# Sums over the partitions in the mixer: one 32-bit matmul becomes two float32r matmuls

## The reference

```
h   = layernorm(x) * (1 + ca) + sa
q, k, v = split(rms(h) @ w_qkv.T);  q = rms(q);  k = rms(k)
y   = sigmoid(q) * cumsum(exp(k) * v) / (cumsum(exp(k)) + 1e-6)
u, g = split(y @ w_swiglu.T)
x   = x + ga * (h + (u * silu(g)) @ w_out.T)
```

## Time and profile before

| | us |
|---|---|
| median of 3 runs | 2037.17 |
| lowest and highest | 2035.51, 2041.21 |
| span of the profiled execution | 2036.9 |
| PE busy in the span | 1888.6 (93%) |
| DVE, ACT, POOL busy | 1382.7, 921.8, 959.1 |
| mixer, steady: PE busy from 450 to 600 | 148.00 of 150 |

### The profile page before, as it was taken

The page is one execution under the profiler, slowest core; times in us unless marked ns, Lnnn a source line. Parts: engine busy times, 40 slices in busy tenths (PEclk is TensorE's granted clock), DMA queues, the critical chain, the costliest instruction groups (busy, mean ns, idle before and its releaser), DMA issues. The chain is left out here.

```text
span 2036.9 us, 25294 instructions
## 1 busy us (share of the span) xinstructions
PE 1888.6 (93%) x8376; PEld 826.3 (41%) x8376; DVE 1382.7 (68%) x1795; ACT 921.8 (45%) x1421; POOL 959.1 (47%) x680
## 2 busy tenths in 40 slices
PE   4638999999999999999999999998999999999996
PEld 1213444444444444444444444443443433433432
DVE  6996884884874866777678457245657768768756
ACT  4445334333423433523432421122776776776773
POOL 0553422421522521431441231213889889989974
PEclk7869999999999999999999999998999999999998
DMA  8223012012012012101101101313101011011011
GB/s 308 83 68 95 24 35 81 11 39 93 5 40 95 6 35 67 40 26 54 62 26 37 60 6 47 112 35 127 63 1 63 22 42 63 22 42 62 0 42 62
DMA packets 62147, 112.06 MB, mean 55 GB/s; under 512 B 4464, under 2 KB 20848, under 8 KB 61424
## 3 DMA queue, kind: packets, MB, share of 16 engines
q1 hardware_dynamic: 62064, 111.06, 16.3%
HBM read 80.11 MB, written 30.93 MB: 55 GB/s over the span
## 5 line engine op out<-in xcount | busy, mean ns | idle before, releaser
L532 PE MATMUL bank<-Y,wsw 128*128 128x512 f16 x3072 | 684.0, 379 | 8.7 <-DVE late L843 8.4
L786 POOL TENSOR_TENSOR late<-late 128x512 f16<-128x512 f32 x128 | 192.1, 1501 | 633.1 <-ACT late L661 633.0
L532 PEld LDWEIGHTS bank<-Y,wsw 128*128 128x128 f16 x3072 | 299.0, 98 | 376.6 <-DVE late L843 12.0
L1621 DVE SCALAR_TENSOR_TENSOR f_A<-bank,gu_s,f_A 128x512 f32<-128x512 f32 x352 | 260.7, 741 | 177.8 <-ACT f_A L1445 166.8
L509 PE MATMUL bank<-late,wout 128*128 128x512 f16 x1536 | 352.4, 379 | 3.6 <-POOL late L786 3.5
L1445 ACT ACTIVATE f_A<-bank,gu_s 128x512 f32<-128x512 f32 x352 | 241.6, 687 | 157.6 <-PE bank L1370 139.1
L487 PE MATMUL bank<-H,wqkv 128*128 128x512 f16 x1152 | 260.1, 387 | 37.0 <-DVE H L868 30.9
L1525 POOL TENSOR_TENSOR f_A<-f_A 128x512 f32<-128x512 f32 x176 | 253.9, 1443 | 72.9 <-DVE f_A L1621 72.4
L1335 PE MATMUL bank<-f_HH,f_down_hi 128*128 128x512 f16 x704 | 267.3, 382 | 20.2 <-POOL f_HH L1535 19.7
L843 DVE TENSOR_TENSOR late<-late,bank 128x512 f32<-128x512 f32 x128 | 87.7, 685 | 227.4 <-PE bank L532 206.8
L653 ACT ACTIVATE late<-bank 128x512 f32<-128x512 f32 x128 | 76.4, 597 | 350.1 <-PE bank L532 265.5
(11 more groups left out here) (151 smaller groups left out, 2143.8 us busy)
## 6 DMA issues: line engine op xcount, KB each, us to landing
room<-packed SPq DMA_DIRECT2D x48, 176.0 KB, 2.4
X<-xT SPq DMA_DIRECT2D x8, 1024.0 KB, 6.0
h_scratch<-X SPq DMA_DIRECT2D x8, 1024.0 KB, 4.2
f_X<-x_scratch SPq DMA_DIRECT2D x8, 1024.0 KB, 5.5
f_N<-x_scratch SPq DMA_DIRECT2D x7, 1024.0 KB, 5.5
outT<-f_X SPq DMA_DIRECT2D x7, 1024.0 KB, 4.2
late<-xT SPq DMA_DIRECT2D x24, 256.0 KB, 2.9
HR<-h_scratch SPq DMA_DIRECT2D x24, 256.0 KB, 3.2
```

Source lines behind the costliest of these rows:

```text
L532: mm = nc.tensor.matmul(out[:], wsw[:, pw, k, col:col + P], Y[:, px, k, :], start=(k == 0 and pw == 0 and px == 0), stop=(k == DT - 1 and ...
L786: nc.gpsimd.tensor_tensor(UG[:, j % 2, 1, :], G, UG[:, j % 2, 0, :], ALU.subtract).then_inc(UG_low, 1)
L1621: nc.vector.scalar_tensor_tensor(a, EV[ev_bank(j, m)][:], gu_s[:, which * I_T + j, g:g + 1], a, ALU.mult, ALU.add).then_inc(by_dve, 1)
```

## The change

`reduce` no longer multiplies the 32-bit tile `RS`. GpSimd writes the sum twice more: once as a float32r tile `RH`, by repeating the last addition with a float32r output just ahead of the ordinary one (`round_sum`), and once as the rest `RL = RS - RH` (`rest_of_sum`) after it. TensorE then does two float32r matmuls that accumulate in the same bank. The first waits for `sum_high`, the second for `sum_low`. `ones_r` is a float32r copy of `ones`. This is done in the 39 reductions of the mixer; block 0's three and those of the second half stay as they are.

```
+            def round_sum(kind, b, last):
+                f = FAMILY[kind]
+                nc.gpsimd.tensor_tensor(RH[f][:], RS[f][:], last, ALU.add).then_inc(sum_high[f], 1)
+            def rest_of_sum(kind, b):
+                f = FAMILY[kind]
+                pool.wait_ge(sum_high[f], parted(kind, b) + 1)
+                nc.gpsimd.tensor_tensor(RL[f][:], RS[f][:], RH[f][:].bitcast(F32), ALU.subtract).then_inc(sum_low[f], 1)
...
                 for c in range(2, DT):
+                    if c == DT - 1:
+                        round_sum(kind, b, SQ[f][:, c % 2, :])
                     nc.gpsimd.tensor_tensor(RS[f][:], RS[f][:], SQ[f][:, c % 2, :], ALU.add).then_inc(sq_sum[f], 1)
+                pool.wait_ge(sq_sum[f], 3 * use + 3)
+                rest_of_sum(kind, b)
...
-                if kind == MEAN:
-                    pe.wait_ge(tile_sum, 3 * (b + 1))
-                else:
-                    pe.wait_ge(sq_sum[f], 3 * (nth_squares(kind, b) + 1))
+                pe.wait_ge(sum_high[f], parted(kind, b) + 1)
                 bank_read(kind, b)
-                nc.tensor.matmul(sum_bank(kind, b)[:], ones[:], RS[f][:], start=True, stop=True).then_inc(reduced[f], 1)
+                nc.tensor.matmul(sum_bank(kind, b)[:], ones_r[:], RH[f][:], start=True, stop=False)
+                pe.wait_ge(sum_low[f], parted(kind, b) + 1)
+                nc.tensor.matmul(sum_bank(kind, b)[:], ones_r[:], RL[f][:], start=False, stop=True).then_inc(reduced[f], 1)
```

More of the change, by code:

```diff
@@ L18 @@
 F32 = mybir.dt.float32
+F32R = mybir.dt.float32r
 F16 = mybir.dt.float16
@@ L61, in program @@
         ones = keep("ones", [P, P], F32)
+        ones_r = keep("ones_r", [P, P], F32R)
         eps = keep("eps", [P, 3], F32)
@@ L91, in mixer @@
     mod, ones, eps, bank = v["mod"], v["ones"], v["eps"], v["bank"]
+    ones_r = v["ones_r"]
     SA, CA, GA, GB = v["SA"], v["CA"], v["GA"], v["GB"]
@@ L121, in mixer @@
         RS = [sb("RSx", [P, T], F32), sb("RSqk", [P, T], F32)]
+        RH = [sb("RHx", [P, T], F32R), sb("RHqk", [P, T], F32R)]
+        RL = [sb("RLx", [P, T], F32R), sb("RLqk", [P, T], F32R)]
         RD = sb("RD", [P, 2, T], F32)
@@ L146, in reductions, with parted @@
             return (3, 2)[FAMILY[kind]] * b + NTH[kind]
+        def parted(kind, b):
+            return reductions(kind, b) - (3 if FAMILY[kind] == 0 else 0)
         def nth_squares(kind, b):
@@ L181, in mixer @@
         reduced = [sem("x_reduced"), sem("qk_reduced")]
+        sum_high = [sem("x_sum_high"), sem("qk_sum_high")]
+        sum_low = [sem("x_sum_low"), sem("qk_sum_low")]
         centred = sem("centred")
@@ L775, in add_x @@
                     pool.wait_ge(tile_sum, 3 * b + c - 1)
+                    if c == DT - 1:
+                        round_sum(MEAN, b, X[:, c, :])
                     nc.gpsimd.tensor_tensor(rs, rs, X[:, c, :], ALU.add).then_inc(tile_sum, 1)
+                pool.wait_ge(tile_sum, 3 * b + 3)
+                rest_of_sum(MEAN, b)
             def weigh(b):
@@ L1064, in _ @@
             nc.vector.memset(ones[:], 1.0 / (DT * P)).then_inc(mod_step, 1)
+            nc.vector.memset(ones_r[:].bitcast(F32), 1.0 / (DT * P)).then_inc(mod_step, 1)
             nc.vector.memset(eps[:, 0:1], v["LN_EPS"]).then_inc(mod_step, 1)
@@ L1068, in _ @@
             nc.vector.memset(run[:], 1.0).then_inc(mod_step, 1)
-            dve.wait_ge(mod_step, 5)
+            dve.wait_ge(mod_step, 6)
             nc.vector.memset(clamped[:], 0.0).then_inc(const_ready, 1)
@@ L1092, in _ @@
             inverse(VAR, 0)
-            dve.wait_ge(mod_step, 6)
+            dve.wait_ge(mod_step, 7)
             s1_modulate(0)
@@ L1106, in _ @@
             add_one(mod[:, CB])
-            clamp(mod[:, GA], 7)
-            clamp(mod[:, GB], 11)
+            clamp(mod[:, GA], 8)
+            clamp(mod[:, GB], 12)
             split_low(6)
@@ L1690 @@
     arrays = {name: np.ascontiguousarray(a) for name, a in arrays.items()}
-    nc = bacc.Bacc("TRN2", target_bir_lowering=False, num_devices=1)
+    nc = bacc.Bacc("TRN2", target_bir_lowering=False, num_devices=1, dynamic_dma_scratch_size=1024)
     args = [nc.dram_tensor(name, a.shape, mybir.dt.from_np(a.dtype), kind="ExternalInput").ap() for name, a in arrays.items()]
```

## The result

| | before | after |
|---|---|---|
| median, us | 2037.56 | 2086.26 |
| lowest and highest, us | 2035.51, 2041.21 | 2085.31, 2088.53 |
| span of the profiled execution, us | 2036.9 | 2083.5 |
| period of a full iteration (from one KSQ reduction to the next), us, five | 162.03 each | 166.9, 167.0, 167.1, 168.7, 167.2 |

The change makes the kernel slower: 1.0238 times [1.0223, 1.0253] the time before. The direction and most of the places were as predicted; the size was not. The profiled span grew by 46.6 us where 24.5 were forecast.

The account below looks back on a forecast made before the run. PE was taken to bound the steady mixer, DVE's chain the part before the pipeline. Five iterations 9.0, ends 6.4 and pre-pipeline 9.1 sum to 24.5 us on 2036.9: about 2061, range 2041 to 2085.

Parts of the forecast that it names:

- What PE gains: Each reduction: two float32r matmuls of 0.216 us replace one 32-bit of 0.86, gaining 0.43; 16.8 us at most over 39.
- KSQ's delay: Full iteration: KSQ's second matmul waits for the rest tile, G(0) +0.45 us, absorbed in PE's 1.50 us wait at U(2).
- What POOL's operations cost: Two more POOL operations a reduction, 1.3 us each where DVE is quiet, bounded by 1.16 and 1.94.
- MEAN: Full iteration: POOL's added operations slow DVE's one-input decoding; U(2) +1.2 us, +0.75 after the reduction's gain; bounds -0.5, +1.9.
- piece (a): Before the pipeline: DVE's modulation products, 1.75 us beside POOL's additions and 0.68 alone; the second part's 16 end 3.6 later.
- VAR: Full iteration: two more POOL operations, 1.94 and 1.5 us, delay low(4); output(4) starts +1.45 us, bounds +0.9 and +2.8.
- Before the pipeline: Five reductions with POOL and DVE in use: 6.5 us late at block 1's qkv, 9.1 in sum, between 4 and 14.
- Piece (e): First qkv before the pipeline: POOL's two split_low lie behind QSQ 1, delaying the next weights and ACT's copy: +2.6 us.
- The ends: First and last iterations, POOL's work straight onto PE: b=0 3.6, last 2.35, one before 0.45; together 6.4, between 4 and 11.
- A: Rival: PE's gain stays and POOL's work hides; 2020 us, chance 0.09.
- B: Rival: gain and delays cancel, prologue doesn't reach PE, DVE's chunk isn't slowed; 2041 us at the middle, chance 0.10.
- C: Rival: POOL's float32r output costs 1.94 us everywhere, +23, 2085; dearer matmuls add up to 8 or some 30; chance 0.13.

Follow-up runs that it names:

- e3: The changed kernel with only QSQ and HSQ of the pipeline's iterations split (13 sums), the rest by the 32-bit matmul; 2035.54 us, 0.9988 of the kernel before.
- e6: The changed kernel with only KSQ of blocks 1 to 7 split, the other sums by the 32-bit matmul; 2040.27 us, 1.0011 of the kernel before.
- e14: The changed kernel with matmuls of unused result: ten ahead of U(2), six between VAR's two matmuls, two ahead of output(4); 2076.05 us, 1.0187.
- e7: The changed kernel with DVE's first decoding chunk moved one step later, behind hidden(1); 2073.83 us, 1.0178.
- e9: The changed kernel with ten 16-bit matmuls of unused result ahead of U(2) in each of seven iterations; 2083.33 us, 1.0217.
- e12: The changed kernel with MEAN's and VAR's rest made behind the low that PE waits for, their matmul pairs behind the following output; 2065.11 us, 1.0136.
- e13: e12 with DVE's first decoding chunk also moved one step later, as in e7; 2058.78 us, 1.0101.
- e11: The changed kernel with the sums of blocks 0 and 1 left to the 32-bit matmul, 32 of 39 split; 2079.62 us, 1.0198.
- e1: The changed kernel without the rest: POOL's last addition writes the float32r tile, one float32r matmul follows; 2022.80 us, 0.9923.
- e2: The changed kernel with all of POOL's work and the wait for the rest tile, but the old 32-bit matmul of RS; 2089.53 us, 1.0262.
- e4: The changed kernel with only MEAN of the pipeline's iterations split (7 sums), the rest by the 32-bit matmul; 2059.70 us, 1.0110 of the kernel before.
- e5: The changed kernel with only VAR of the pipeline's iterations split (7 sums), the rest by the 32-bit matmul; 2054.70 us, 1.0079 of the kernel before.
- e10: e1 (no rest, one float32r matmul a sum) with DVE's first decoding chunk also moved one step later; 2020.26 us, 0.9904.
- e8: The kernel before, with no split, with DVE's first decoding chunk moved one step later, behind hidden(1); 2029.38 us, 0.9960.

## Why the prediction was right or wrong

**What PE gains: right.** 0.47 for the pair against 0.43, a gain of 0.39 a reduction. QSQ and HSQ keep it (e3), KSQ's delay hides for the most part in the wait at U(2) (e6), as the steps said. G(0) behind KSQ came 0.65 later in the iteration where 0.45 was forecast.

**What POOL's operations cost: right while DVE is quiet.** 1.27 against the 1.3 taken.

**MEAN: the mechanism was right, the term of 1.2 us was mis-sized; it is 2.1.** The prediction let only one-input operations end with POOL's and "the two-input ones between" run free. Blocked were L982 (953 in the kernel before), with two inputs in SBUF, 0.51 to 1.59, and L983 (954) behind it by another 1.07; L990 (961), which the step had named, kept its 0.34. That is 2.15 us where 1.28 were worked out, and 4.4 us in five iterations. The Trainium skill ("GPSIMD Engine Reference", Key points) names instructions with two SBUF inputs beside the 2-port modes; L982 agrees with it. The trace before showed this half too: the prediction's own piece (a) takes a DVE product of two SBUF inputs at 1.75 us beside POOL and 0.68 alone, and the step for MEAN did not use it.

**VAR: 1.45 forecast, 2.2 measured.** A rest of 1.5 was assumed in the middle of a scan; all three operations were beside it and took 2.06, 2.18 and 1.98. That is 3.9 us in five iterations. The price of 1.94 beside the scan had been read from the earlier trace rows and not used for all of them.

**The step that was missing: what a longer wait does to the clock.** The forecast added waits as waits. 9.1 of the 26.8 us are no waits: PE works at 1.2 GHz behind a wait of 2.93 us, or behind the two of 1.46 and 0.70 (e14). The step put this at nothing and gave no reason. The page before could have warned: the kernel's steady waits were 1.50 us at most at a granted clock of 1.00, and the step moved one to about 2.3 and made a new one. With these three, 4.4 + 3.9 + 9.1, and 0.4 for the somewhat dearer pairs, the five iterations' excess of 17.8 us is accounted for.

**Before the pipeline.** 7.3 against 6.5 at block 1's `qkv`: right. Piece (e), the first `qkv` behind it, was 5.0 and not 2.6. There a second wait for ACT and one of 1.81 for the rest tile came up, 3.9 us more of waits, and a second fall, which adds 1.0 us; which of the two late chains counts was not separated. Part of it belongs to this execution: e7, e9, e12, e13 and e14 have the same start and reach the first gate group at 185.7 to 186.3, some 10 us later than the kernel before, not 12.3. That b=0 takes less when the start is late (e11) had not been seen either.

**The ends.** b=0 3.3 against 3.6, in which a fall of 1.3 took the place of part of the wait; b=6 and b=7 2.3 more than forecast, of which 1.1 is the fall behind MEAN at 1347.93 (3.82 instead of 2.75).

**The rivals.** A (POOL's work hides) and B (it cancels) are out. C gave 2085, near the measured time, but by another way: it priced POOL's float32r output at 1.94 everywhere, and undisturbed it costs 1.27 (e1). Its surcharges for a dearer matmul, 8 and some 30 us, don't follow from its prices either (39 reductions at 0.43 or 1.29 more are 17 and 50 at most), but nothing hangs on them. What was dear is every POOL operation beside DVE's scans, whatever its output, and DVE's operations beside POOL's. That the number agrees is chance. The time lies 1 us above the end of the range: the bound of 21 us for the five iterations held no term for the clock.

**What stays open.** Which wait the clock falls behind. In the five full iterations the 2.93 us at U(2) is followed by a fall in four cases in the kernel after, in one of e2 and in none of e11, and e4's still longer wait of 3.64 us in two. The waits of 1.46 and 0.70 at `output(4)` are followed by one in two cases in the kernel after, in one of e5, in four of e7 and in all five of e9 and of e11. No single steady wait of up to 1.9 us was followed by one (the kernel before, e1, e12, e13). What besides the wait's length decides was not found. Executions of one kernel differ in it too: in e13 and e10 the one that was over 5 us faster had the higher granted clock.

## What to carry to other kernels

Work moved off a full engine is paid by the engine that takes it and, here, by DVE, whose operations beside it end late: list what both do beside the added operations, and let every one of those end late, the two-input ones too. Then look which waits of TensorE grow: one that grows from 1.5 to about 3 us can cost half as much again behind it, and hiding one such wait may only hand the fall to the next. Put the added operation behind what TensorE waits for (e12 gained 21 us that way), and move other work out of its neighbourhood first, which here paid even without the change (e8).

## What the runs showed of the hardware

- A float32r matmul of 512 columns costs 0.25 us by starts (e1), a pair 0.47, a 16-bit one 0.216, a 32-bit one 0.86. Each float32r matmul has one record, with a weight load of 0.19.
- POOL's tensor-tensor operation of 512 elements takes 1.27 us with a float32r output as with a 32-bit one, and 2.0 to 2.2 beside DVE's scan.
- DVE's operations of 352 elements that started while POOL added ended 0.2 to 0.4 us behind POOL's operation: 1.41 us instead of 0.30 with one input, 1.59 instead of 0.51 with two in SBUF. e2 repeats it (1.58) with the same POOL work, and e1, without POOL's two additional operations, is back at 0.51; a pair of such operations by itself wasn't measured.
- A fall of TensorE's granted clock behind a short wait cost 1.1 to 1.7 us in a stretch of 12 matmuls (2.75 us at 2.4 GHz), and in the first such stretches of e4 up to 2.5. Matmuls of unused result in the waits took the falls away (e14).
